# Graph network kernel: in the gather passes VectorE puts up to three one-hot comparisons between the four sums of a group

## The reference, cut to what matters

```python
agg = jax.ops.segment_sum(h[src] * norm[:, None], dst, n)            # twice, 64 and then 64 wide ("narrow")
agg = jax.ops.segment_sum(x[src], dst, n)                            # once, 128 wide
for l in range(5):                                                   # five times, 128 wide
    m = jax.nn.relu(h[src] + edge_attr)
    agg = jax.ops.segment_sum(m, dst, num_segments=n)
```

## Time and profile before

| | |
|---|---|
| median of three runs | 11315.0 us |
| profiled execution, its own time | 11327.94 us |
| its span, first to last instruction | 11326.1 us |
| busy: PE, DVE, ACT, POOL | 76%, 67%, 56%, 68% |
| mean granted TensorE clock | 0.881 of full speed |
| span at the five edge passes (windows of 979 to 988 us) | 4922 us |
| span at the three sum passes | 2806 us |

### The profile page before, as it was taken

The page is one execution under the profiler, slowest core; times in us unless marked ns, Lnnn a source line. Parts: engine busy times, 40 slices in busy tenths (PEclk is TensorE's granted clock), DMA queues, the critical chain, the costliest instruction groups (busy, mean ns, idle before and its releaser), DMA issues. The chain is left out here.

```text
span 11326.1 us, 289319 instructions
## 1 busy us (share of the span) xinstructions
PE 8557.2 (76%) x56134; PEld 6362.2 (56%) x56140; DVE 7582.3 (67%) x21898; ACT 6355.2 (56%) x16870; POOL 7714.8 (68%) x7879
## 2 busy tenths in 40 slices
PE   4888688688868886887788688868886666655665
PEld 2777577555545554665565465646564555545554
DVE  6777677555556666776667666667775566746667
ACT  4444454444455556555555555555555676646774
POOL 2777777677757766775777577757773777557774
PEclk7999799799979998999899899989997778868887
DMA  2111111222234434443444344434433666446663
GB/s 57 31 31 30 38 32 31 51 56 56 55 94 111 109 91 114 112 110 90 116 111 111 95 111 109 113 94 112 110 107 104 182 193 193 143 135 188 197 196 109
DMA packets 1311535, 1169.02 MB, mean 103 GB/s; under 512 B 239258, under 2 KB 1106238, under 8 KB 1310224
## 3 DMA queue, kind: packets, MB, share of 16 engines
q0 software_dynamic: 272544, 566.00, 19.9%
q1 hardware_dynamic: 1038256, 596.28, 18.1%
HBM read 1009.04 MB, written 152.40 MB: 103 GB/s over the span
## 5 line engine op out<-in xcount | busy, mean ns | idle before, releaser
L1412 POOL DMA_INDIRECT rings<-rows_key,idx x4536 | 4365.8, 962 | 1913.8 <-issue 1330.1
L1596 DVE TENSOR_TENSOR bigDE<-bigDE,part 128x128 f32 (+1 forms) x6656 | 1891.3, 284 | 1405.2 <-PE part L1507 424.6
L1507 PE MATMUL part<-rings 128*128 128x128 f32 (+1 forms) x11920 | 1713.4, 290 | 655.8 <-ACT rings L1448 242.9
L1520 PE MATMUL wide<-bigDE,bigC 128*128 128x384 bf16 x10800 | 1951.8, 338 | 249.0 <-DVE bigC L1578 238.7
L692 POOL DMA_INDIRECT bigDE<-rows_key_value,idx x1664 | 1647.3, 990 | 692.0 <-issue 654.3
L1507 PEld LDWEIGHTS part<-rings 128*128 128x128 f32 (+1 forms) x11920 | 1558.1, 190 | 833.6 <-issue 759.9
L1439 ACT ACTIVATE rings<-iota,relK 128x128 f32<-128x128 f32 x5960 | 1900.2, 389 | 4.9 <-issue 1.5
L1412 POOL DMA_INDIRECT rings<-rows_hidden,idx x1424 | 1389.2, 976 | 595.4 <-issue 406.2
L1431 ACT COPY idx<-srcK 128x4 int32 (+1 forms) x1490 | 283.6, 191 | 2516.4 <-PE part L1507 2333.1
L1520 PEld LDWEIGHTS wide<-bigDE,bigC 128*128 128x128 bf16 x10800 | 1071.7, 101 | 988.3 <-issue 397.3
L1578 DVE TENSOR_SCALAR bigC<-bigC,node 128x512 bf16<-128x512 int16 x4410 | 1386.1, 379 | 45.4 <-issue 42.8
(11 more groups left out here) (372 smaller groups left out, 10319.2 us busy)
## 6 DMA issues: line engine op xcount, KB each, us to landing
rings<-in_attr SPq DMA_DIRECT2D x3780, 64.0 KB
walk_value<-bigDE SPq DMA_DIRECT2D x416, 256.0 KB
rings<-walk_value SPq DMA_DIRECT2D x416, 256.0 KB
rings<-rows_key,idx POOLq DMA_INDIRECT x4536
bigDE<-rows_key_value,idx POOLq DMA_INDIRECT x1664
bigF<-in_attr SPq DMA_DIRECT2D x380, 64.0 KB
rings<-rows_hidden,idx POOLq DMA_INDIRECT x1424
rows_key<-rings SPq DMA_DIRECT2D x60, 320.0 KB, 2.6
```

The costliest lines, as they stand in the source:

```text
L1412: e.indirect_dma_start(to[:, r, 0:width], None, table, bass.IndirectOffsetOnAxis(ap=idx[:, r:r + 1], axis=0)).then_inc(gate.sem, 16)
L1507: last = e.matmul(part[0:width, bank(n), r, :], msg[:, r, 0:width], sel[:, r, :], start=True, stop=True)
L1520: last = e.matmul(wide[:, r, 0:3 * width], hot[:, r * P:r * P + P], room.pieces(s, 1).rearrange("p a j f -> p (a j f)"), start=s == 0, sto ...
L1596: e.tensor_tensor(into, into, got, ALU.add).then_inc(c.added.sem, 1)
```

## The change

In `steps` the comparisons of `blocks(n)` are split. All but the last three stay where they were, ahead of the join. The last three are kept back and issued one after each of the first three sums of group n, that is, behind the join of group n + 2 and behind the wait for the product of group n. The number of instructions that compute, and what each waits for, are the same; TensorE's, ScalarE's, GpSimd's and SyncE's order are untouched.

```diff
             def steps(i, numbers, last=False):
                 for n in numbers:
+                    mine = []
                     if place(n + 1)[1] is None:
                         prepare(i, n + 1)
                     if not isinstance(i, int) or i >= 0:
-                        for half, s in blocks(n):
+                        mine = blocks(n)
+                        for half, s in mine[:-3]:
                             hot(i, half, s)
                     else:
...
                     _hold(e, c.product, q_of(i, n) + 1, c.tick_dve)
                     for r in range(GROUP):
                         add(i, n, where[(n - skip) % 2 * GROUP + r], r)
+                        for half, s in mine[-3:][r:r + 1]:
+                            hot(i, half, s)
```

## The result

| | before | after |
|---|---|---|
| median of runs, us | 11316.49 (11312.64 to 11328.23, 4 runs) | 11518.58 (11512.14 to 11522.85, 4 runs) |
| span of the profiled execution | 11326.1 | 11521.0 |
| VectorE busy, whole span | 7582 | 7247.1 |

The change makes the kernel slower: ratio 1.0174, 95% interval 1.0161 to 1.0186, 202 us on the medians and 194.9 on the spans. I had forecast 11434, in a range that ended at 11500. The direction was right, the size was not.

The account below looks back on a forecast made before the run. The prediction took GpSimd's gathers, at a fixed 1.25 us distance, as the bound, with merges deciding when they go on in edge passes. 11327.9 + 119 + 0 = 11447, on the median 11434; range 11340 to 11500.

Parts of the forecast that it names:

- Where the waits arise: Edge passes: TensorE waits for comparisons in mid-portion behind two expansions; GpSimd's index waits grow from 21 to some 45 us a pass.
- The term of 119 us: Five edge passes: late merges lengthen GpSimd's index waits by 2.65 us a round, 24 a pass, 119 in all.
- Its split: Per edge-pass round: the merge in the middle 1.05 us later, the merge at the round's end 1.6 us later.
- the weight I gave the joins: Edge passes: kept-back comparisons stand behind the join of n + 2, which waits for a DMA; two gated joins underlie the 1.6 us.
- I take 0 for these three passes: Wide sum pass and two narrow passes: no join, TensorE has leading expansions to do, so 0 us change.
- VectorE's saving: On VectorE, a sum and comparison pair takes 0.57 us instead of 0.72, saving 0.43 us per group.
- Rival 1: No overlap on VectorE: a pair takes 0.72 us, 3.55 us a round, 160 a kernel, 11475; chance 0.12.
- Rival 2, the clock: Edge passes: TensorE's new pauses lower its clock at two positions a round, 243 us on top, 11677; chance 0.06.
- Rivals 3 and 4: 3: edge-pass lateness taken up by reserve, 11315, chance 0.11. 4: index copies come before GpSimd asks, 11257, chance 0.10.
- rival 4: Fetch behind each edge-pass merge: VectorE catches up sooner, index copies come early, gaining at most 58 us, 11257; chance 0.10.

Follow-up runs that it names:

- behind_join: Against the kernel before: in edge passes only, the last three comparisons stand behind the join but ahead of the product wait and the sums; 11386.85 us, ratio 1.0059.
- forward: Against the kernel before: in all passes the next position's first three comparisons, not this one's last three, stand between the sums; 11294.68 us, ratio 0.9967.
- micro2: No computation: 96 gathers each beside bursts of one comparison, six, one join, six comparisons from PSUM, with 2 to 4 sums between; gather means 953, 969, 1071, 946 ns.

## Why the prediction was wrong, step by step

- *Where the waits arise*: right. TensorE pauses behind two expansions for L1578, in rows of 8 and 12 matmuls, and GpSimd waits at the merges.
- *The term of 119 us*: measured 125, so right in size. Its split was off. Merge to merge, mean of the edge passes, the way from the middle of a round to its end grew from 46.96 to 48.43, the other from 55.06 to 57.07: 1.5 and 2.0 us, 0.7 of the sum being longer gathers, where I had 1.6 and 1.05. Also off was the weight I gave the joins: behind_join shows the wait for the product and the place between the sums to be the greater part of the waits. That two errors in the split nearly cancel is luck.
- *"I take 0 for these three passes"*: the step that failed, with its forecast "in the sum passes nothing, with 945 us of gathers and gaps as before". They cost 34 us, and the same term, missing for the edge passes too, cost 30 there: the gathers themselves got longer, in passes where nobody waits as in those where somebody does. I took a gather's 0.94 us for fixed and asked only who waits for whom. The page of before already had gathers of 962 ns on average beside a usual 944, so some of them were longer, and I didn't ask beside what. The bound that I gave the sum passes, 0 to 11 us for the wide one by a late handoff, named another mechanism and left the narrow ones out.
- *VectorE's saving*: right in sign, greater than I said. A pair takes 0.46 at the least and 0.51 on average, not 0.57: the comparison starts 0.20 after the sum, inside its 0.28, and the sum 0.26 to 0.27 after the comparison. Rival 1 (0.72 for every pair) is refuted; of the 29 of 504 that take 0.70 or more, 13 have a comparison of over 0.5 us, as the one of 0.58 above, begun 0.46 to 0.55 after a gather's start.
- *Rival 2, the clock*: refuted. The granted clock over the first edge pass is 0.92, as it was before (the last number but two of the window rows), and the 12 matmuls behind a pause take 2.11 us, 0.176 each, as the earlier trace rows has it for 12.
- *Rivals 3 and 4*: refuted for this change. The gain of rival 4 exists, and forward shows what is left of it, 37 us; it needs comparisons that come early. There the waits of the five edge passes fall by 52 us, and longer gathers take 31 back.

The Trainium skill has the rule that I left out, in SBUF — State Buffer, section Who interferes with whom: GpSimd has only VectorE's second pair of SBUF ports, a `tensor_scalar` in a two-port mode takes that pair exclusively, and a DMA issued from GpSimd needs it to write its descriptors (the write side of this, the section says, is inferred). The runs agree for the comparison from SBUF (114 ns on average, begun 80 to 120 ns ahead) and for that from PSUM (nothing). By that rule alone one would not have got the size: it doesn't say when in a gather the pair is needed. For two SBUF inputs the section infers that descriptor writing isn't held up, and it also says that such an instruction contends with a GpSimd instruction that reads SBUF. Here joins lengthened gathers by up to 0.52 us in micro2. These gathers take their row numbers from SBUF (`idx`), so the second rule may be the one that applies; no run separates the two.

That the ports are the way by which a comparison lengthens a gather is argued from that page. The runs show the dependence on the comparison's start and on its input, int16 in SBUF or fp32 in PSUM. With the memory the number type and the comparison's length (374 or 742 ns) changed too; a comparison of fp32 in SBUF was not run.

## What to carry to other kernels

An operation moved between others on an in-order engine causes no wait only if it comes no later than its reader wants it: take work from the next step forward, not work of this step back. And where one engine's fixed-length instruction is the floor of a stage, look at its mean against its usual length first; what lengthens it is a term of any change to the engine beside it, even where nobody waits.

## What was not expected of the hardware

A single comparison from SBUF delays a gather only in a narrow phase. Gathers that start 60 to 200 ns behind one are longer by up to some 220 ns less that distance (132 ns was the most in micro2, at 80 to 100 ns); at other distances micro2 shows nothing. Within a run of comparisons the delay can be the whole run, and in the narrow passes gathers that start outside that band are held too. GpSimd in the first narrow pass of the changed kernel:

```profile
398.61 0.94 POOL L1412 DMA_INDIRECT rings<-rows_hidden,idx  x1 [0.30 <-issue]
399.85 2.66 POOL L1412 DMA_INDIRECT rings<-rows_hidden,idx  x1 [0.30 <-issue]
402.82 0.95 POOL L1412 DMA_INDIRECT rings<-rows_hidden,idx  x1 [0.30 <-issue]
```

and VectorE there:

```profile
399.78 0.60 DVE L1578 TENSOR_SCALAR bigDE<-W,node 128x512 bf16<-128x512 int16 x2
400.30 1.39 DVE L1578 TENSOR_SCALAR rings<-W,node 128x512 bf16<-128x512 int16 x5
401.91 0.28 DVE L1596 TENSOR_TENSOR bigDE<-bigDE,part 64x128 f32 x1 [0.22 <-issue]
```

Seven comparisons follow one another 0.26 us apart; the gather starts 0.07 behind the first and ends 0.82 behind the end of the last. Gathers of 2.6 to 2.7 us stand 21 times in the narrow passes of the changed kernel, and the bursts of six in micro2 gave none over 1077 ns. What makes a run hold the gather so long is open.

The comparison costs 374 ns with int16 in SBUF and 742 with fp32 in PSUM, and in a run those from SBUF start 0.26 us apart, less than their own length, those from PSUM 0.66 (3.38 us for five).
